# One reciprocal for the row sums of two query tiles, in every second slot of a softmax pipeline

## What is computed

```python
q = (x @ w_q)...; k = (x @ w_k)...; v = (x @ w_v)...        # 32 query heads, 8 key/value heads, HD = 128
lq = x @ w_lq; lk = (lq @ w_lk)...; lv = (x @ w_lv)...      # 32 latent heads
q, k, lk = rope(q), rope(k), rope(lk)
attn = _causal_attn(q, k, v, SCALE)      # softmax(mask(q k^T * scale)) v
lat  = _causal_attn(q, lk, lv, SCALE)
return attn @ w_o + lat @ w_lo
```

## Time and profile before

| | before |
|---|---|
| median of 3 runs | 2185.76 us |
| the profiled execution | 2185.91 us |
| its span, first to last instruction | 2184.1 us |
| what lies around the span | 1.8 us |
| mean granted TensorE clock | 0.992 |
| busy share of the span: PE, PEld, DVE, ACT, POOL | 96%, 89%, 64%, 48%, 41% |

### The profile page before, as it was taken

How to read it: one execution, slowest core, us unless ns; L and a number is a source line. 1 busy time by engine, 2 the same in 40 slices (tenths; PEclk the granted TensorE clock), 3 DMA queues, 4 the chain that set the end, 5 groups by cost and what they waited for, 6 DMA issues and landing times.

```text
span 2184.1 us, 44663 instructions
## 1 busy us (share of the span) xinstructions
PE 2102.7 (96%) x14928; PEld 1951.9 (89%) x14928; DVE 1404.9 (64%) x3734; ACT 1040.6 (48%) x2501; POOL 886.7 (41%) x769
## 2 busy tenths in 40 slices
PE   6999999999999999999999999999999999999995
PEld 6989999898998989999899998989999898998983
DVE  4656757576575656757567575666756577575765
ACT  2544626355263643726346263553626446263551
POOL 3434434344353434435344353444434344353430
PEclk9999999999999999999999999999999999999997
DMA  4010010100001010010100001010010000100001
GB/s 154 1 32 11 2 53 1 42 1 34 20 1 42 2 42 11 2 42 1 53 1 11 32 2 52 2 32 11 1 53 2 32 11 20 34 1 30 1 11 39
DMA packets 15511, 50.60 MB, mean 23 GB/s; under 512 B 1696, under 2 KB 3744, under 8 KB 15136
## 3 DMA queue, kind: packets, MB, share of 16 engines
q1 hardware_dynamic: 15264, 47.47, 6.4%
HBM read 45.37 MB, written 2.10 MB: 22 GB/s over the span
## 4 chain that ended last, share of the span: by engine, by line
PE 44%; issue 33%; POOL 19%; DVE 2%; POOLq 1%; ACT 0%; DVEq 0%; ACTq 0%
POOL probs L630 13%; PE ps L270 13%; PE ps L271 12%; PE ps L272 12%; PE ps L358 5%; POOL probs L625 4%; POOL pt_lo L611 2%; PE ps L332 1%; DVE pt_lo L637 1%; DVE stats L781 0%; ACT pt_hi L475 0%; PE ps L453 0%; POOLq L629 0%; PE ps L468 0%; POOL wlk_lo L617 0%
## 5 line engine op out<-in xcount | busy, mean ns | idle before, releaser
L630 POOL TENSOR_TENSOR probs<-probs,inv_sum 128x640 f32<-128x640 f32 (+7 forms) x512 | 586.6, 1147 | 691.7 <-DVE inv_sum L724 690.9
L637 DVE TENSOR_TENSOR pt_lo<-ps,pt_hi 128x512 fp32r<-128x512 f32 (+3 forms) x768 | 401.6, 551 | 185.9 <-ACT pt_hi L475 182.7
L507 ACT ACTIVATE probs<-probs,neg_max 128x640 f32<-128x640 f32 (+7 forms) x512 | 397.6, 777 | 165.3 <-DVE neg_max L717 165.3
L475 ACT ACTIVATE pt_hi<-ps 128x512 fp32r<-128x512 f32 (+3 forms) x768 | 347.0, 486 | 168.7 <-PE ps L358 155.2
L717 DVE CUSTOM_DVE_ANT_0 probs<-ps,mask 128x640 f32<-128x640 f32 (+7 forms) x512 | 383.8, 752 | 59.7 <-PE ps L272 43.1
L270 PE MATMUL ps<-pt_hi,x_hi 128*128 128x256 f32 x1280 | 377.7, 295 | 9.4 <-POOL wlk_lo L617 9.4
L272 PE MATMUL ps<-pt_hi,x_lo 128*128 128x256 f32 x1280 | 363.4, 284 | 0.0
L271 PE MATMUL ps<-pt_lo,x_hi 128*128 128x256 f32 x1280 | 362.8, 283 | 0.0
L358 PE MATMUL ps<-ident,probs 128*128 128x128 f32 x2304 | 336.7, 274 | 9.6 <-POOL probs L630 8.0
L358 PEld LDWEIGHTS ps<-ident,probs 128*128 128x128 f32 x2304 | 267.2, 140 | 41.0 <-DVE pt_lo L637 19.6
L270 PEld LDWEIGHTS ps<-pt_hi,x_hi 128*128 128x128 f32 x1280 | 245.7, 192 | 12.3 <-POOL wlk_lo L617 9.8
(11 more groups left out here) (110 smaller groups left out, 4654.2 us busy)
## 6 DMA issues: line engine op xcount, KB each, us to landing
raw<-wo SPq DMA_DIRECT2D x32, 512.0 KB, 3.3
raw<-wq SPq DMA_DIRECT2D x16, 512.0 KB, 3.3
raw<-wlv SPq DMA_DIRECT2D x16, 512.0 KB, 4.1
raw<-wkv SPq DMA_DIRECT2D x8, 512.0 KB, 3.5
acc<-xT SPq DMA_DIRECT2D x4, 512.0 KB, 5.9
acc<-x SPq DMA_DIRECT2D x1, 2048.0 KB, 7.8
wlk_raw<-wlk SPq DMA_DIRECT2D x16, 128.0 KB, 3.1
out<-acc SPq DMA_DIRECT2D x8, 256.0 KB, 2.4
```

Of the source, the lines that this page charges most:

```text
L475: return nc.scalar.activation(dst, src, ACT.Copy)
L507: nc.scalar.activation(dst, dst, ACT.Exp, bias=neg_max[:, n % 4:n % 4 + 1], scale=-1.0, accum_out=row_sum[:, n % 4:n % 4 + 1]).then_inc(q[ ...
L630: nc.gpsimd.tensor_tensor(b, b, inv_sum[:, k % 4:k % 4 + 1].to_broadcast([P, w]), ALU.mult).then_inc(q["normed"], 1)
L637: return nc.vector.tensor_tensor(dst, src, h, ALU.subtract)
```

## The change

The function `inverse`, which takes the reciprocal of one column of `row_sum`, becomes `inverse_of_two`, which takes those of tiles n and n + 1 in one instruction, after the exponentials of both, and raises `inverted` by 2. Tiles 0 and 1 have theirs where they had it. Of the later tiles, slot k has had the reciprocal of tile k - 1; now the even slots have those of tiles k - 2 and k - 1, and the odd slots have none. The other engines' lists are as they were.

```diff
-            def inverse(g, pair, n):
-                dve.wait_ge(q["exped"], per_pair(g, pair, TILES, n + 1))
-                nc.vector.reciprocal(inv_sum[:, n % 4:n % 4 + 1], row_sum[:, n % 4:n % 4 + 1]
-                                     ).then_inc(q["inverted"], 1)
+            def inverse_of_two(g, pair, n):
+
+                dve.wait_ge(q["exped"], per_pair(g, pair, TILES, n + 2))
+                nc.vector.reciprocal(inv_sum[:, n % 4:n % 4 + 2], row_sum[:, n % 4:n % 4 + 2]
+                                     ).then_inc(q["inverted"], 2)
...
                             for n in range(EARLY):
                                 row_max(g, pair, n)
-                            for n in range(EARLY):
-                                inverse(g, pair, n)
+                            inverse_of_two(g, pair, 0)
...
                         if EARLY + MID <= k < TILES:
                             row_max(g, pair, k)
-                        if EARLY <= k - 1 < TILES:
-                            inverse(g, pair, k - 1)
+                        if EARLY <= k - 2 < TILES and k % 2 == 0:
+                            inverse_of_two(g, pair, k - 2)
```

## The result

The changed kernel takes 2647.64 us in the median of 4 runs (2645.78 to 2653.6), the kernel before 2186.07 us: 1.212 times as long, with a 95% interval of 1.210 to 1.214. The profiled execution took 2653.6 us, against 2185.9 us before. The forecast was 2585 us, in a range of 2490 to 2690.

What follows compares the result with a forecast made beforehand. PE, busy 96% of the span, was taken to bound the kernel. Stalls of 321.1 us on the profiled 2185.9 us gave 2507.0 us; clock falls of 78.4 us made it 2585.4 us, range 2490 to 2690.

Steps and rivals of the forecast that it cites:

- DVE's saving is worth 0: On DVE, 256 of 512 reciprocals go, 41 us, but the saving lands in a wait for ACT.
- The stalls: PE waits for late normalised tiles: place 6 133.0, place 2 116.6 and 34.1, tile 30 31.0, place 4 6.4 us.
- The split between place 4 and `pt_lo`: At place 4, lateness up to 0.47 us against a vanishing 0.30 us `pt_lo` wait; 0.1 taken, 64 times: 6.4 us.
- the two thirds that I gave them: PE's wait for `pt_lo`, 28.3 us before, should fall by up to two thirds.
- the 290 to 320 that I had named: PE's wait for POOL at the turns: from 8.0 us in 16 times to 290 to 320 us in about 128 to 190.
- half of the 112: TensorE's clock falls after 56 of the 64 longest and 48 next stalls, at 1.4 us each: 78.4 us.
- the upper bound of 179: TensorE's clock falls after each of the 128 stalls: 179 us at most.
- The clock that stays: Rival: the stalls come but TensorE's clock does not fall, 2507 us; chance 0.18.
- A fall after nearly every stall: Rival: TensorE's clock falls 112 to 128 times, 2664 to 2686 us; chance 0.14.
- The sign that I had named for it: A mean granted clock of 0.90 or below would show that the clock falls after nearly every stall.
- only the tiles of 1024 columns stall: Rival: stalls at place 6 and tile 30 only, 133 + 31 us, 2350 us; chance 0.05.
- that none does: Rival: no tile stalls PE, and the waits for `pt_lo` may go, 2157.6 us; chance 0.04.

Runs made afterwards that it cites:

- run 1: Kernel before, with two single one-column reciprocals one behind the other in the even slots instead of one of two columns: 2649.73 us.
- run 7: Changed kernel, with PE turning the identity matrix 14 or 16 times before it waits for tiles with n % 4 == 2, results unused: 2504.48 us.
- run 10: Kernel before, with place 4's exponential moved behind place 2's upper parts on ACT and its reciprocal between probs_lo(place 2) and place 6's maximum on DVE: 2152.51 us.
- run 9: Changed kernel, with the pair's reciprocal ahead of the row maximum of its even slot instead of behind it: 2384.71 us.
- run 6: Kernel before, with only tiles 6/7 modulo 8 sharing a reciprocal, the others keeping single ones in their old slots: 2401.12 us.
- run 5: Kernel before, with only tiles 2/3 modulo 8 sharing a reciprocal, the others keeping single ones in their old slots: 2360.07 us.

## Why the prediction was right, and what it got wrong

**DVE's saving is worth 0: right.** The 256 reciprocals that went bought nothing (run 1 has all 512 and takes as long), and two columns take 0.160 us. The 41 us that they were to take off DVE were too much: its busy time is 15 us below that of run 1 (1401.0 against 1416.3 us).

**The stalls: right, in their places and their sizes.** The median distances between the starts of two turns, over the second and third step of each of the 16 passes (place 7 to 0 goes into the next step):

| distance of turns | before | changed | run 7 (clock up) | forecast |
|---|---|---|---|---|
| place 1 to 2 | 0.80 | 3.24 | 3.17 | +2.43 |
| place 3 to 4 | 3.30 | 3.59 | 3.59 | +0.1 |
| place 5 to 6 | 0.92 | 3.70 | 3.62 | +2.77 |
| place 2 to 3, and 6 to 7 | 2.73, 3.33 | 4.36, 4.93 | 2.78, 3.38 | 0 |
| place 4 to 5, 7 to 0, 0 to 1 | 1.67, 3.57, 1.80 | 1.70, 3.42, 1.78 | 1.69, 3.41, 1.78 | 0 |
| a whole step | 18.11 | 26.71 | 23.43 | +5.3 |

With the clock held up, a step is 5.32 us longer, and 5.3 was the forecast. That the two agree so closely is partly luck: place 4 comes 0.3 us later instead of 0.1, and the way from place 7 to place 1 of the next step is 0.18 us shorter, though the forecast said that nothing is won back. The forecast sum of the stalls was 321 us; measured are 334.4 - 23.6 = 311 us by the waits of the changed kernel, and 2504.5 - 2185.3 = 319 us by run 7. The split between place 4 and `pt_lo` was off: PE waits 0.6 to 0.7 us at place 4, where I had 0.1 net (by the distances it is 0.3), and the waits for `pt_lo` went by more than the two thirds that I gave them. That is why the 190 waits add up to 342 us, above the 290 to 320 that I had named.

**The clock: the right mechanism, under-sized.** This is the step of the sum that failed: "I take half of the 112: 56 x 1.4 = 78.4 us". The trace has 93 falls after stalls, 44 of the 48 at place 2 in later steps (2.3 us idle), 49 of the 64 with 2.6 us of idle time, and none of the 16 at tile 30 (1.6 to 1.7 us idle). Most of the error is their number: 93 instead of 56, at 1.4 us each, are 52 of the 79 us. The rest is their price: each lasted 3.4 us, not the 3.0 that I could see of one before, and by PE's busy time it cost 1.7 us instead of 1.4, 157.7 us in all, inside the upper bound of 179. By the 149 us between the profiled executions of the changed kernel and of run 7 it cost 1.6. The stalls 10 us less and the clock 79 us more make 2654 us, which is the profiled execution.

**The rivals.** The clock that stays (2507 us) is what run 7 builds and measures, at 2504.5 us, and is not what the changed kernel does. The Trainium skill's rule (TensorE: Matmul & The Clock Gate, "HAM oscillation — how this bites in real kernels") would have led to that number; here the measurement decides against it, since all of the falls came after shorter gaps than the page warns of. A fall after nearly every stall (2664 to 2686 us) was closer than the forecast in its number of falls and in its time (16 us off, the forecast 62), but a quarter of the longest stalls had none. The sign that I had named for it, a mean granted clock of 0.90 or below, could not have shown it: by an estimate from the trace before (0.992) and half of 3.4 us lost per fall, even 128 falls leave 0.91. Measured is 0.934. That only the tiles of 1024 columns stall is refuted by the wait of 2.29 us at place 2 of the changed kernel, where place 6 stalls as well; that none does, by every wait above.

## What to carry to other kernels

Before moving an instruction by one slot of a software pipeline, follow the path through the engines from the consumer's last turn to its next, link by link: the same delay was free at place 0, cost 43 us with place 4 and 403 us at places 2 and 6. An instruction saved on an engine that idles in that path buys nothing; what is worth moving is what stands ahead of something that the bounding engine waits for, as run 10 shows. And a stall on TensorE of about 2 us or more should be priced with what it does to the clock, here half as much again.

## What the hardware did that I had not expected

- The clock fell after idle times of PE of 1.9 to 2.0 us, too: 19 of 64 in run 9, where none of the 64 of 1.2 to 1.7 us was followed by a fall, and 8 of the 16 at tile 30 in run 6. It is not the length alone. Stalls of 2.3 us were followed by a fall 44 times in 48 in the changed kernel and 24 times in 48 in run 5, those of 2.6 us 49 times in 64 and 27 times in 48 (run 6). In the changed kernel and in runs 5 and 6, the falls after stalls of 2.3 us and more began between 0.7 us before and 1.6 us after PE resumed. What decides it in each case is left open.
- 14 to 16 useless turns of the identity in each stall made the kernel 143 us faster than leaving PE idle.
